# A decoder layer on one core: the state times the queries moves to VectorE, the sums over pairs of chunks to GpSimd, and steps of the attention to other places

## The reference, cut to what matters

```python
def step(S, inp):                       # attn: S is a 16x16 state for each of 4 x 16 heads
    qt, kt, vt, at, gft = inp
    bs1 = einsum('bhk,bhkv->bhv', kt, S)
    S1 = S + at[..., :, None] * bs1[..., None, :]
    S2 = exp(gft)[..., None] * S1
    bs2 = einsum('bhk,bhkv->bhv', kt, S2)
    S3 = S2 + at[..., :, None] * bs2[..., None, :] + kt[..., :, None] * vt[..., None, :]
    o = einsum('bhk,bhkv->bhv', qt, S3)
    return (S3, o)
_, o = scan(step, S0, ...)              # 1024 steps, one after another
out3 = stack([z, z, o], axis=2).reshape(B, 3 * N, H, HD)     # z are zeros
out = out3[:, -N:].reshape(B, N, D)     # so only the outputs of the last third of the steps are used
out = out * sigmoid(x @ Wo1 @ Wo2); out = (out - mu) * rsqrt(var + 1e-5) * ln_w; return out @ Wout
# cross attention: softmax(q k^T / 4) v, 16 heads, then @ Wo.T + bo
# experts: 2 shared and 8 routed (two of the 8 for each token), 256 -> 1024 -> 256 with gelu
```

## Time and profile before

| | |
|---|---|
| median of 3 runs | 2462.38 us (2462.02 to 2462.51) |
| profiled execution, its time | 2462.45 us |
| its span (first to last instruction) | 2460.7 us |
| DVE busy | 2098.7 us (85%) |
| PE busy | 1771.4 us (72%) |
| POOL busy | 1146.7 us (47%) |
| ACT busy | 665.3 us (27%) |
| L1586 copy of the state, 171 times | 54.8 us, 320 ns each |
| L1548 sum of the products, 171 times | 82.2 us, 481 ns each |
| L1169 product on POOL, 171 times | 147.6 us, 863 ns each |

### The profile page before, as it was taken

How to read it: one execution, slowest core, us unless ns; L and a number is a source line. 1 busy time by engine, 2 the same in 40 slices (tenths; PEclk the granted TensorE clock), 3 DMA queues, 4 the chain that set the end, 5 groups by cost and what they waited for, 6 DMA issues and landing times.

```text
span 2460.7 us, 31859 instructions
## 1 busy us (share of the span) xinstructions
PE 1771.4 (72%) x9438; PEld 1335.1 (54%) x9438; DVE 2098.7 (85%) x5941; ACT 665.3 (27%) x1457; POOL 1146.7 (47%) x1228
## 2 busy tenths in 40 slices
PE   4258987998599859986898350267886569866993
PEld 2135765676467746775667230144674436754683
DVE  5999999899989998999899999998999979953000
ACT  2131234213421332133313020161222611223221
POOL 2544453565446544654484468264562763214103
PEclk8567998899889988998899765567998669976997
DMA  8000342344234423442334230000354003530243
GB/s 262 27 5 11 127 137 80 103 141 138 76 101 141 138 78 99 143 138 77 99 108 164 75 100 9 20 1 3 101 190 143 18 1 107 191 130 18 99 166 111
DMA packets 175109, 238.51 MB, mean 97 GB/s; under 512 B 28657, under 2 KB 148074, under 8 KB 174954
## 3 DMA queue, kind: packets, MB, share of 16 engines
q1 hardware_dynamic: 140874, 194.46, 23.6%
q10 hardware_dynamic: 27936, 25.44, 3.3%
q0 software_dynamic: 6144, 16.79, 2.1%
HBM read 202.09 MB, written 33.16 MB: 96 GB/s over the span
## 4 chain that ended last, share of the span: by engine, by line
DVE 64%; PE 15%; issue 8%; POOL 8%; DMA 3%; ACT 2%; SPq 0%; POOLq 0%; ACTq 0%; DVEq 0%; PEldq 0%
DVE ps L1594 13%; DVE ps L1575 12%; DVE prod L1567 10%; DVE terms L1582 8%; DVE terms L1577 5%; PE ps L630 3%; PE ps L639 3%; PE ps L523 3%; DVE rec_out L1523 2%; DVE rec_in L1523 2%; PE ps L521 2%; DVE stats L1283 1%; DVE SE_out L1586 1%; POOL y_back L1046 1%; PE ps L575 1%
## 5 line engine op out<-in xcount | busy, mean ns | idle before, releaser
L1594 DVE TENSOR_REDUCE ps<-terms 128x64 f32<-128x320 f32 x1024 | 451.5, 489 | 0.0
L1575 DVE TENSOR_REDUCE ps<-prod 128x16 f32<-128x272 f32 x1024 | 400.0, 438 | 0.0
L1582 DVE TENSOR_TENSOR terms<-ps,rec_out 128x256 f32<-128x256 f32 x1024 | 384.5, 420 | 0.0
L1567 DVE TENSOR_TENSOR prod<-ps,rec_in 128x256 f32<-128x256 f32 x1024 | 383.7, 419 | 0.0
L630 PE MATMUL ps<-xg,fc 128*128 128x128 f32 x2848 | 357.1, 286 | 33.6 <-PE ps L639 13.3
L630 PEld LDWEIGHTS ps<-xg,fc 128*128 128x128 f32 x2848 | 347.2, 201 | 56.0 <-issue 48.3
L639 PE MATMUL ps<-pj,hT 128*128 128x256 f32 x1424 | 342.7, 395 | 34.7 <-ACT hT L919 34.7
L639 PEld LDWEIGHTS ps<-pj,hT 128*128 128x128 f32 x1424 | 272.0, 196 | 89.7 <-ACT hT L919 53.6
L1169 POOL TENSOR_TENSOR oprod<-SE_out,rec_q 128x320 f32<-128x320 f32 x171 | 147.6, 863 | 354.3 <-DVE SE_out L1586 353.4
L566 PE MATMUL ps<-xtf,fc 128*128 128x512 f32 x512 | 241.6, 609 | 8.1 <-ACT hT L870 4.7
L575 PE MATMUL ps<-pj,hT 128*128 128x256 f32 x1024 | 240.0, 386 | 0.0
(11 more groups left out here) (234 smaller groups left out, 2964.3 us busy)
## 6 DMA issues: line engine op xcount, KB each, us to landing
fc<-in_wfcT SPq DMA_DIRECT2D x80, 1024.0 KB, 5.2
pj<-in_wpT SPq DMA_DIRECT2D x80, 1024.0 KB, 8.7
xg_rows<-in_rows ACTq DMA_DIRECT2D x105, 128.0 KB, 2.1
out_rows<-y ACTq DMA_DIRECT2D x89, 128.0 KB, 5.7
in_rows<-o_rows SPq DMA_DIRECT2D x2, 2176.0 KB, 17.3
out_rows<-o_rows SPq DMA_DIRECT2D x2, 2176.0 KB, 17.0
xtp<-in_xT SPq DMA_DIRECT2D x32, 128.0 KB
xin<-in_x SPq DMA_DIRECT2D x8, 512.0 KB, 6.8
```

Source lines behind the costliest of these rows:

```text
L1567: tt(prod[:, c % PLACED, :, cols, 0:HD], SE[:, old, cols, 0:HD].unsqueeze(1).to_broadcast([P, NV, HC, HD]), rec_in[:, c].unsqueeze(2).to_b ...
L1575: red(SE[:, old, cols, HD:EH].rearrange("p v n -> p n v"), prod[:, c % PLACED, :, cols, 0:HD + 1], AX.X, ALU.add).then_inc(step_done, 1)
L1582: tt(terms[:, cols, :, 0:NV], SE[:, old, cols, HD:EH].unsqueeze(2).to_broadcast([P, HC, HD, NV]), rec_out[:, c].unsqueeze(1).to_broadcast( ...
L1594: red(SE[:, new, cols, 0:HD], terms[:, cols, :, 0:NV + 1], AX.X, ALU.add).then_inc(step_done, 1)
```

## The change

DVE no longer copies the state: at the same place it multiplies it, read from PSUM, by the queries into `oprod`, which now has room for four chunks. POOL no longer multiplies; after every second chunk it adds up the products of two chunks in five steps (20 columns to 4, 8, 4, 2 and 1). DVE's multiply of a pair waits for the sums of the pair before the last one. `fk` takes the place of a column block of `vec` that is free at that time. On TensorE the projection `finish` comes an expert later. The places of the steps in both tables change, and in the tail the last layer norm of tile 6 comes after the routing and the scatters of tile 7.

```diff
-        fk = sb("fk", [P, CH, D])
+        fk = vec[:, :, E_COL]
-        SE_out = sb("SE_out", [P, 2, HV, EH])
-        oprod = sb("oprod", [P, 2, CH, HV, EH])
+        oprod = sb("oprod", [P, 2 * PAIR, CH, HV, EH])
...
+        def pairs_before(sb_at):
+            return (sb_at - KEEP) * (NCH // PAIR) - SKIPPED // PAIR if sb_at > KEEP else 0
+        def pair_of(sb_at, c):
+            return pairs_before(sb_at) + c // PAIR - (SKIPPED // PAIR if sb_at == KEEP else 0)
... TensorE
-                def second_and_finish():
-                    second()
-                    finish()
-                last_experts(f, (start, attend, weigh, second_and_finish, lambda: None))
+                last_experts(f, (start, attend, weigh, second, finish))
... GpSimd, steps
-                def output_terms(c):
-                    pool.wait_ge(copied, kept_before(sb_at) + (c + 1))
-                    tt(oprod[:, c % 2], SE_out[:, c % 2].unsqueeze(1).to_broadcast([P, CH, HV, EH]),
-                       rec_q[:, c].unsqueeze(2).to_broadcast([P, CH, HV, EH]), ALU.mult).then_inc(o_terms, 1)
+                def output_sums(c):
+                    first = max(c // PAIR * PAIR, SKIPPED if sb_at == KEEP else 0)
+                    nth = pair_of(sb_at, c)
+                    part = oprod[:, first % (2 * PAIR):c % (2 * PAIR) + 1].rearrange("p r i v e -> p (r i v) e")
+                    pool.wait_ge(o_terms, kept_before(sb_at) + (c + 1))
+                    if sb_at > KEEP and c == 1:
+                        pool.wait_ge(o_ready, sb_at - KEEP)
+                    tt(part[:, :, 0:NV], part[:, :, 0:NV], part[:, :, HD:EH], ALU.add).then_inc(o_tree, 1)
+                    pool.wait_ge(o_tree, nth * 4 + 1)
+                    tt(part[:, :, 0:8], part[:, :, 0:8], part[:, :, 8:16], ALU.add).then_inc(o_tree, 1)
...
+                    tt(osum[:, first:c + 1]..., part[:, :, 0], part[:, :, 1], ALU.add).then_inc(o_sums, 1)
-                    if keep and is_kept(sb_at, c):
-                        output_terms(c)
+                    if keep and is_kept(sb_at, c) and c % PAIR == PAIR - 1:
+                        output_sums(c)
... GpSimd, tail
-            normalize(LN_3, 6, y_out, y_out)
             rsqrt(LN_2, 7)
             for i in range(MOVES):
                 scatter(7, i)
+            normalize(LN_3, 6, y_out, y_out)
... VectorE
-            def outputs(sb_at, c):
-                dve.wait_ge(o_terms, kept_before(sb_at) + (c + 1))
-                red(osum[:, c], oprod[:, c % 2], AX.X, ALU.add).then_inc(o_sums, 1)
+            def output_terms(sb_at, c, state):
+                if pair_of(sb_at, c) > 1:
+                    dve.wait_ge(o_sums, pair_of(sb_at, c) - 1)
+                tt(oprod[:, c % (2 * PAIR)], state.unsqueeze(1).to_broadcast([P, CH, HV, EH]),
+                   rec_q[:, c].unsqueeze(2).to_broadcast([P, CH, HV, EH]), ALU.mult).then_inc(o_terms, 1)
-                        nc.vector.tensor_copy(SE_out[:, c % 2], SE[:, old]).then_inc(copied, 1)
+                        output_terms(sb_at, c, SE[:, old])
-                    if keep and c and is_kept(sb_at, c - 1):
-                        outputs(sb_at, c - 1)
-                outputs(sb_at, NCH - 1)
-                dve.wait_ge(o_sums, kept_before(sb_at + 1))
+                dve.wait_ge(o_sums, pairs_before(sb_at + 1))
-                last_stats(t, 6, BOUND_AT["divisors"])
+                last_stats(t, 6, BOUND_AT["scatter"] + 8)
-FREE_AT = {1: 1, "caps": 46, "minima": (40, 42, 43, 44), "sums": (50, 51, 52, 54), "divisors": 55, "divided": 60, "resid": 71, 2: 71, "routing": 84, "gather": 82, "scatter": 93, "combine": 101, 3: 109}
-BOUND_AT = {"gated": 3, 0: 3, "x_plus": 10, 1: 10, "minima": (18, 18, 19, 20), "sums": (34, 34, 35, 35), "divisors": 36, "divided": 40, "resid": 44, 2: 44, "routing": 54, "gather": 28, "scatter": 63, "combine": 46, 3: 51}
+FREE_AT = {1: 1, "caps": 46, "minima": (40, 42, 43, 44), "sums": (48, 48, 49, 50), "divisors": 51, "divided": 55, "resid": 73, 2: 73, "routing": 85, "gather": 82, "scatter": 94, "combine": 101, 3: 110}
+BOUND_AT = {"gated": 3, 0: 3, "x_plus": 12, 1: 13, "minima": (22, 22, 23, 24), "sums": (40, 40, 41, 41), "divisors": 42, "divided": 46, "resid": 53, 2: 53, "routing": 63, "gather": 30, "scatter": 74, "combine": 50, 3: 57}
```

More of the change, by code:

```diff
@@ L58 @@
 PLACED = 4
+PAIR = 2
 EH = HD + NV
@@ L210, in decoder_layer @@
          pool_set, pool_const, dve_const, ctx_k_ps, ctx_v_ps, ctx_done, prep_a_ps, prep_b_ps, xf1_sb, fq_sb,
-         kv_sb, sum_seen, prep_pool, block_laid, v_placed, step_done, decayed, copied, o_terms, o_sums, o_ready,
+         kv_sb, sum_seen, prep_pool, block_laid, v_placed, step_done, decayed, o_terms, o_tree, o_sums, o_ready,
          cap_done, x1T_ps, x1T_sb, q_ps, q_sb, sc_ps, sc_sb, capped, min_done, shifted, exp_done, summed, eT_ps,
@@ L219, in decoder_layer @@
             pool_set pool_const dve_const ctx_k_ps ctx_v_ps ctx_done prep_a_ps prep_b_ps xf1_sb fq_sb kv_sb
-            sum_seen prep_pool block_laid v_placed step_done decayed copied o_terms o_sums o_ready cap_done x1T_ps x1T_sb q_ps q_sb sc_ps sc_sb capped min_done shifted exp_done summed eT_ps eT_sb rden_done widened
+            sum_seen prep_pool block_laid v_placed step_done decayed o_terms o_tree o_sums o_ready cap_done x1T_ps x1T_sb q_ps q_sb sc_ps sc_sb capped min_done shifted exp_done summed eT_ps eT_sb rden_done widened
             attT_ps spread_ps spread_sb attT_sb wo_ps resid x2T_ps doubled x2T_sb rt_ps rt_sb route w_done picked
@@ L1165, in steps @@
                 first = PREP_FROM_SECOND if sb_at % R else PREP_FROM_KEPT if keep else PREP_FROM
-                def output_terms(c):
-                    pool.wait_ge(copied, kept_before(sb_at) + (c + 1))
-                    tt(oprod[:, c % 2], SE_out[:, c % 2].unsqueeze(1).to_broadcast([P, CH, HV, EH]),
-                       rec_q[:, c].unsqueeze(2).to_broadcast([P, CH, HV, EH]), ALU.mult).then_inc(o_terms, 1)
+                def output_sums(c):
[8 more added lines that the diff above has]
+                    tt(part[:, :, 0:8], part[:, :, 0:8], part[:, :, 8:16], ALU.add).then_inc(o_tree, 1)
+                    pool.wait_ge(o_tree, nth * 4 + 2)
+                    tt(part[:, :, 0:4], part[:, :, 0:4], part[:, :, 4:8], ALU.add).then_inc(o_tree, 1)
+                    pool.wait_ge(o_tree, nth * 4 + 3)
+                    tt(part[:, :, 0:2], part[:, :, 0:2], part[:, :, 2:4], ALU.add).then_inc(o_tree, 1)
+                    pool.wait_ge(o_tree, nth * 4 + 4)
+                    tt(osum[:, first:c + 1].rearrange("p n i v -> p (n i v)"), part[:, :, 0], part[:, :, 1], ALU.add).then_inc(o_sums, 1)
                 pool.wait_ge(block_laid, laid_before(sb_at + 1))
                 for c in range(NCH):
-                    if keep and is_kept(sb_at, c):
-                        output_terms(c)
+                    if keep and is_kept(sb_at, c) and c % PAIR == PAIR - 1:
+                        output_sums(c)
                     for at_t, job in jobs:
```

## The result

The changed kernel takes 2433.97 us (median of 4 runs, 2432.36 to 2437.06) against 2462.2 us (4 runs, 2461.14 to 2462.51). The ratio is 0.9888 with a 95% interval of 0.987 to 0.9905: 28 us faster, where 13 were forecast. The time lies inside the forecast range; the gain is a little over twice the forecast one. The profiled execution took 2432.66 us, its span is 2430.7.

A forecast was written before the change was run, and what follows sets the result against it. DVE's recurrence was taken as the main bound, with TensorE nearly level in periods 6 and 7. Savings of 8 (free tiles), 3 (period 5), 1.5 (bound tiles) and 1.3 (tail) made 13.8 us: 2449 us, range 2432 to 2466.

The forecast's parts named there:

- The multiply, the pair on POOL: Kept chunks: DVE's multiply takes 0.40 us, saving 0.224 us a chunk; POOL's sums take 2.5 us a pair.
- Super-block 11's waits: Period 5: DVE waits 13 us for POOL's sums, giving back the chunks' savings there; 3 us gained in the period.
- Free tiles: Periods 0 to 4: expert ahead of the projection, which takes 9.0 us; DVE's waits fall from 38.5 to 30.3, 8 us saved.
- a row and a rule: Projection's length: profile row of 12.7 us at clock 0.50, against the skill page's activity rule, near 6.3; 9.0 taken.
- rival 2: Projection behind the expert is granted the high clock: 2438 us; chance 0.14.
- Periods 6 and 7: Bound tiles: TensorE's lateness makes DVE wait and cancels nearly all chunk savings; 1.5 us gained, bounds -8 to +15.
- rival 1: DVE's saving arrives whole, 38 us, plus half of POOL's waits and the free tiles' 8: 2409 us; chance 0.14.
- Tail: After the last expert: moving tile 6's combination wait off the division gains 1.3 us; its late layer norm is hidden.

The follow-up runs named there:

- b_filler: The kernel before, plus 16 matmuls of 256 columns whose result nothing reads, ahead of the projection in periods 2 to 4: 2441.35 us.
- e_bound: The changed kernel with the table of step places for periods 6 and 7 as before the change: 2406.14 us.
- c_outputs: The kernel before with only DVE's multiply and POOL's sums of pairs; TensorE order, both tables and tail as before: 2430.7 us.
- i_lag: The changed kernel with routing part 5 in periods 6 and 7 due at t = 63 again instead of 71: 2419.93 us.
- g_jobs: The changed kernel with POOL's norms, gathers and combinations of a chunk ahead of the sums of a pair: 2421.46 us.
- k_tail: The kernel of e_bound with tile 6's last norm back ahead of tile 7's scatter and its variance at the divisors: 2411.43 us.
- a_order: The changed kernel with TensorE doing the projection ahead of expert 8 again, tables staying changed: 2439.53 us.

## Why the prediction was wrong

**The multiply, the pair on POOL: right.** 0.40 us from start to start as taken (0.17 to 0.29 saved); a kept chunk is 3.41 us at the median (before it was 3.64, not 3.66). 2.5 us a pair. Super-block 11's waits are 1.69, 1.43, 1.53, 4.53, 2.37, 11.5 us for 13 forecast; period 5 gained 5.1 instead of 3, inside its ends.

**Free tiles: the step that failed.** "Now it follows dense matmuls instead of idleness, so part of it may be granted the high clock: I take 9.0, between 6.3 and 12.7." The projection took 6.8, all at 2.4 GHz, in each of four periods: 2.2 us each, 8.8 in sum. Its place was reckoned right: in period 2 it started at 674.7, where 685.4 less the 10.8 us that the period began earlier makes 674.6. The waits forecast for periods 2 to 4 were 7.7 us each; less 2.2 they are 5.5, and the trace has 5.57, 4.67 and 6.10 (period 1 4.07 for 5.3, period 0 1.90 as forecast). I had taken the middle between a row and a rule because the row showed 12.7 us of projection that did not raise its own clock. That row says nothing on a projection that dense work leads into, which b_filler shows by itself: same work, same place, filler ahead, 6.8 us. The mechanism was my rival 2, at 0.14. The expert's second half still took 4.9, 6.4, 5.5 and 6.5 us, near the 5.93 of the earlier trace rows: the clock rose only while it ran (in period 2 it is 0.50 from 667.7 to 672.5 and 1.00 from 673.5 on).

The Trainium skill, page "TensorE: Matmul & The Clock Gate", Part 1, says that throttled is the default and activity releases it. The trace agrees at the four places with dense work ahead. In periods 6 and 7 the projection ran 12.7 us at 0.51 with hardly a gap and stayed there: its own activity did not release anything, and the rule taken to mean any activity would have had these two fast as well.

Nor is it enough that the clock is high when the projection starts. In period 7 of e_bound it starts at 1.00, behind the attention's short matmuls and 1.7 us of idleness, and falls to 0.50 on the way; it takes 10.6 us (columns as in the earlier trace rows, all matmuls):

```profile
1922.90:1925.50 2.60, 2.55 (x9) 0.97 0.00 0
1925.50:1933.50 8.00, 8.00 (x16) 0.50 0.01 2
```

The tail's 10.9 us after the change are alike. At the seven places of the changed kernel and b_filler with 6.8 us an expert's half or the filler stood ahead, 16 matmuls of 256 columns each, with 1.8 us of idleness between at most. Which feature of the work ahead keeps the clock up is not shown.

Of the 12 us missing in this term (20.4 against 8), 8 are these waits, and some 5 are likely DVE's small routing operations, which had been stretched in the kernel before (last section) and mostly were no longer. Rival 2's 2438 had the first part of this and not the second.

**Periods 6 and 7: the sum right, the reading wrong.** -1.5 forecast, +1.4 measured. The chain was as I had it: `rstd` waits of 3.05, 2.95, 3.05; residual waits of 2.61 and 2.60 (2.6 forecast); the preparation waiting for routing part 5 past the super-block's end; the tail's turn at TensorE's last expert. Three things in it were not: DVE's wait in period 7 was 7.5 us at the gated rows, not 7 at "x_plus"; LN_2's in period 7 was 9.58, behind a combination on POOL; and the sums of super-block 13 cost 14.8 us that I had not counted at all. The error of reading is larger than these. I took TensorE's short waits for a sign that TensorE is a bound of its own, and the savings of DVE in these periods for lost in any order. c_outputs and e_bound show the contrary: with the old places these periods take 26.6 and 29.0 us less than before. TensorE's lateness was a sum of things that the new places and the sums ahead of POOL's jobs add (i_lag: 14 us with one part moved back; g_jobs: 12.5 with the jobs first), not its work. My rival 1 had the mechanism of these periods right, but not the size of the whole: c_outputs stands at 2430.7 where its whole saving would have given 2412.

**Tail: mis-sized.** 1.3 forecast, 5.9 in the profile, 0 to 5 by the medians of k_tail and e_bound, 10 to 13 between profiles without the pause. The 1.3 was read off an input that had itself been held by the pause of ACT, 5.3 us long in the kernel before. What makes the pause stays open.

Of the 30 us between the two profiled executions (28 by the medians), then, 20 came from the free periods, mostly by the clock, 5 from period 5 and 6 from the tail, and 1 was lost in periods 6 and 7: the 27 to 29 us that the outputs' change brings there were spent on later places and POOL's order.

## What to carry to other kernels

A stretch of matmuls that always runs at the low clock has two prices, and which one holds was settled here by what the engine did just before it: try dense work directly ahead, even work for nothing, before you count it at its old length, and read the granted clock over the whole stretch, not at its start. When an engine waits only a few us at one point, ask whether the work it does before that point was itself late for the same reason; if so the two are one chain and no second bound. When steps in an order written by hand are moved, look at each that another engine waits for and whether it crosses a boundary with a long block behind it; one such step cost 14 us here. And before two tails, or any two stages, are compared by one profile each, look for a pause that one of them has and the other lacks.

## What the runs showed of the hardware

Some of DVE's small operations lasted until a POOL instruction ended. In the kernel before (DVE, then POOL):

```profile
730.51 0.84 DVE L1409 TENSOR_TENSOR lterm<-lower,passes 128x72 f32<-128x72 f32 x1
...
731.65 0.98 DVE L1413 TENSOR_SCALAR first_row<-first_pass 128x8 f32<-128x8 f32 x1
...
729.97 1.28 POOL L1129 TENSOR_TENSOR fk<-fbuf,vec 128x512 f32<-128x512 f32 x1
731.33 1.27 POOL L1130 TENSOR_TENSOR zp<-fk,vec 128x512 f32<-128x512 f32 x1
```

In i_lag the same two operations, with POOL idle:

```profile
1682.35 0.23 DVE L1425 TENSOR_TENSOR lterm<-lower,passes 128x72 f32<-128x72 f32 x1
...
1682.88 0.17 DVE L1429 TENSOR_SCALAR first_row<-first_pass 128x8 f32<-128x8 f32 x1
```

0.84 us against 0.23, ending at 731.35 where POOL's ended at 731.25; 0.98 against 0.17, ending at 732.63 where POOL's ended at 732.60. The second has one input tensor, not two. Counting the operations that took over 0.15 us more than the shortest of their kind, the excess over periods 0 to 4 came to 7.2 us before and 2.2 after; a_order and b_filler, which have the old order on TensorE, keep 7.1 of it in periods 1 to 4. No run took the POOL instruction away by itself, so the cause is read from this coincidence, not shown. The Trainium skill's page "GPSIMD Engine Reference", section "Specifications", has the SBUF interfaces shared with VectorE, with contention for its instructions in a 2-port perf mode or with two SBUF inputs; the first pair of rows fits the second condition, and whether the TENSOR_SCALAR ran in such a mode no row shows.
